# Step one of a two-step graph diffusion: two PSUM copies and the next tile's coarse search levels in another order on ScalarE and GpSimd

## What is computed

```python
def _adj_from_feats(Xa, W1, W2, W3):
    Q = Xa @ W1
    K = Xa @ W3
    logits = Q @ W2 @ K.T / TAU
    idx = jnp.argsort(-logits, axis=1)
    vals = jnp.take_along_axis(logits, idx, axis=1)
    csum = jnp.cumsum(jax.nn.softmax(vals, axis=1), axis=1)
    k_i = jnp.sum(csum < P_NUC, axis=1) + 1          # P_NUC = 0.9
    ...
    masked = jnp.where(keep, logits, -jnp.inf)
    return jax.nn.softmax(masked, axis=1)
...
for s in range(STEPS):                               # STEPS = 2
    A = _adj_from_feats(Xa, W1, W2, W3)
    Xf = Rf @ Xf
    Xb = Rb @ Xb
    Xa = A @ Xa
    Z = Z + (Xf @ U1[s] + Xb @ U2[s] + Xa @ U3[s])
```

## Time and profile before

| what | value |
|---|---|
| median of 3 runs | 2497.32 us (2494.7 to 2497.5) |
| the profiled execution: its own time | 2493.01 us |
| the profiled execution: span | 2491.2 us |
| PE busy | 1956.3 us (79%) |
| DVE busy | 1924.2 us (77%) |
| ACT busy | 1700.4 us (68%) |
| POOL busy | 838.4 us (34%) |
| mean granted TensorE clock | 0.921 of full speed |
| chain that ended last | ACT 21%, issue 13%, POOL 13%, PE 4%, DVE 1% |

### The profile page before, as it was taken

How to read it: one execution, slowest core, us unless ns; L and a number is a source line. 1 busy time by engine, 2 the same in 40 slices (tenths; PEclk the granted TensorE clock), 3 DMA queues, 4 the chain that set the end, 5 groups by cost and what they waited for, 6 DMA issues and landing times.

```text
span 2491.2 us, 33017 instructions
## 1 busy us (share of the span) xinstructions
PE 1956.3 (79%) x10002; PEld 1286.8 (52%) x10002; DVE 1924.2 (77%) x6082; ACT 1700.4 (68%) x1806; POOL 838.4 (34%) x1438
## 2 busy tenths in 40 slices
PE   2999565999999999998548778778778678688693
PEld 1555333666666666666325455445455455455462
DVE  6777658888888888887386887877877878878876
ACT  4434147888888888886367777777777677677640
POOL 2000043444444444444243343333332332333423
PEclk9999887999999999999869989989989989889896
DMA  6777220111111111111510100001001001001013
GB/s 228 286 284 278 103 65 18 49 48 49 49 48 49 48 48 48 48 48 39 180 61 1 39 20 25 34 20 38 20 20 39 20 20 39 20 20 39 19 47 140
DMA packets 65726, 167.62 MB, mean 67 GB/s; under 512 B 7037, under 2 KB 45307, under 8 KB 61947
## 3 DMA queue, kind: packets, MB, share of 16 engines
q1 hardware_dynamic: 65530, 165.43, 19.1%
HBM read 117.95 MB, written 47.45 MB: 66 GB/s over the span
## 4 chain that ended last, share of the span: by engine, by line
ACT 21%; issue 13%; POOL 13%; PE 4%; DVE 1%; POOLq 0%; DMA 0%; ACTq 0%; DVEq 0%; SPq 0%
ACT junk_a L900 10%; ACT junk_a L895 8%; POOL over L808 7%; PE banks L1346 3%; POOL over L816 1%; ACT pt L919 1%; POOL over L811 1%; POOL rough_t L818 1%; POOL points L820 1%; DVE region L1274 1%; POOL minus_t L822 1%; POOL points L814 1%; DVE region L1269 0%; ACT zt L945 0%; PE banks L1338 0%
## 5 line engine op out<-in xcount | busy, mean ns | idle before, releaser
L1346 PE MATMUL banks<-xa,pt 128*128 128x256 f32 x2704 | 683.2, 407 | 232.7 <-ACT pt L919 232.7
L1346 PEld LDWEIGHTS banks<-xa,pt 128*128 128x128 f32 x2704 | 534.0, 204 | 389.1 <-ACT pt L919 245.1
L895 ACT ACTIVATE junk_a<-pb_all,minus_t 128x3327 f16<-128x3327 f32 x151 | 463.9, 3072 | 221.2 <-POOLq L823 220.9
L900 ACT ACTIVATE junk_a<-pb_all,minus_t 128x3327 f16<-128x3327 f32 x151 | 463.0, 3066 | 1.8
L1392 PE MATMUL banks<-region,at 128*128 128x512 f16 x2028 | 448.9, 381 | 0.0
L808 POOL TENSOR_SCALAR over<-over,points 128x1 f32<-128x1 f32 x151 | 104.5, 692 | 881.3 <-ACT junk_a L900 881.2
L1200 DVE TENSOR_SCALAR_CACHE_REDUCE pb_all<-banks 128x1024 f32<-128x1024 f32 x260 | 210.9, 848 | 225.9 <-PE banks L1311 223.7
L1392 PEld LDWEIGHTS banks<-region,at 128*128 128x128 f16 x2028 | 199.1, 98 | 230.1 <-issue 4.1
L1311 PE MATMUL banks<-keys,qs 64*128 64x512 f32 (+1 forms) x832 | 199.9, 577 | 88.4 <-DVE pb_all L1200 49.2
L808 POOL TENSOR_SCALAR over<-over,rough_t 128x1 f32<-128x1 f32 x78 | 185.1, 2373 | 169.2 <-ACT junk_a L900 169.1
L1338 PE MATMUL banks<-ident,pb_all 128*128 128x128 f32 x1352 | 181.6, 281 | 54.5 <-DVE pb_all L1131 34.4
(11 more groups left out here) (222 smaller groups left out, 2859.7 us busy)
## 6 DMA issues: line engine op xcount, KB each, us to landing
at<-adjT_d SPq DMA_DIRECT2D x52, 832.0 KB, 4.8
region<-in_adj_dram SPq DMA_DIRECT2D x25, 1663.5 KB, 8.0
adjT_d<-at SPq DMA_DIRECT2D x26, 832.0 KB, 3.9
fb_d<-fb_sb SPq DMA_DIRECT2D x26, 256.0 KB, 2.0
region<-fb_d SPq DMA_DIRECT2D x2, 3328.0 KB, 19.0
y_d<-y_sb SPq DMA_DIRECT2D x50, 128.0 KB, 1.9
x_d<-pb_all SPq DMA_DIRECT2D x1, 3328.0 KB, 10.4
qs<-q_d SPq DMA_DIRECT2D x104, 32.0 KB, 4.1
```

Of the source, the lines that this page charges most:

```text
L895: nc.scalar.activation(junk_a[:, 0:w], pb[u][:, 0:w], ACT.Relu, scale=sign, bias=t, accum_out=over[u][:, 0:1])\
L900: nc.scalar.activation(junk_a[:, 0:w], pb[u][:, 0:w], ACT.Sign, scale=sign, bias=t, accum_out=over[u][:, 1:2])\
L1346: last = nc.tensor.matmul(bank[4][:, 0:D], pt[sl][:, t * P:(t + 1) * P], xa[:, t0 + t, :], start=(t0 + t == 0), stop=(t0 + t == T - 1))
```

## The change

Two tables and the place of two calls change; all of it is in step one (the entries of step zero stay).

```diff
--- before.py
+++ after.py
@@ -71,7 +71,7 @@
     ROUGH = (0, 3)
     BISECTIONS = (4, 3)
     ACT_BISECTIONS = (3, 3)
-    EARLY_BISECTIONS = (0, 3)
+    EARLY_BISECTIONS = (0, 2)
     AIM = (6.0, 16.0)
     CUT_AIM = (6.0, 24.0)
     VERIFIED = (0, 1)
@@ -853,7 +853,6 @@
                             .then_inc(S2("fb_lo")[k.slot], 1)
                     if not first:
                         level(m, 1)
-                        level(m, 2)
                 step_sweep(pool, body)
                 if not first:
                     pool.wait_ge(sem("scale_in"), 32)
@@ -865,7 +864,7 @@
             def _(act):
                 act.wait_ge(S("search_consts"), 1)
 
-                STEPS = ((), (0,), (1,), (2, 3), (4,), (5,)) if first else ((), (6,), (7,), (8, 9), (10,), (11,))
+                STEPS = ((), (0,), (1,), (2, 3), (4,), (5,)) if first else ((), (4, 5, 6), (7,), (8, 9), (10,), (11,))
                 relus = Chain(act, "step_relu_sum", base=sum(sum(LEVELS[q]) for q in range(s)))
                 signs = {}
 
@@ -967,14 +966,8 @@
                                     .then_inc(S2("sx_lo")[i.slot], 1)
                                 nc.scalar.activation(t256[i.slot][:, n, :], bank[5 + n][:, D:2 * D], ACT.Copy, scale=sc[:, i.t, :])\
                                     .then_inc(S2("sx_lo")[i.slot], 1)
-                                if n == 0 and m.inside(T):
-                                    for q in range(2, 4):
-                                        sums(m, q)
-                    elif not first and m.inside(T):
-                        for q in range(2, 4):
-                            sums(m, q)
                     if not first and m.inside(T):
-                        for n in range(4, 6):
+                        for n in range(2, 4):
                             sums(m, n)
                     if not first and i.static and i.t == T - 1:
                         layernorm_sqrt(act, 2, 0, T - 2)
```

## The result

The changed kernel takes 2532.58 us (median of 4 runs, 2530.62 to 2535.24) against 2497.41 (2494.7 to 2497.89) for the kernel before: 1.0144 times as long, 95% interval 1.0126 to 1.0161, some 35 us more. The direction was forecast; the time lies above the forecast range, which ended at 2529.

The account below looks back on a forecast made before the run. ACT and POOL in turns set the pace. Legs of 27.6 to 28.2 and 18.7 made the period 46.3 to 46.9 against 46.08; over 23 periods 5 to 19, middle 12: 2497.3 + 12 = 2509 us, range 2494 to 2529.

Parts of the forecast that it names:

- the two legs: Period split: first from start of DVE pass L1131 (A) to first fine sum (F), 16.59 us; second F to next A, 28.93.
- F = A + 18.7: First fine sum starts 18.7 us after L1131's start, against 16.59, because POOL's additions and L1064 delay level 2.
- Product 2 starts at F + 4.0: On PE, product 2 starts 4.0 us after the first fine sum's start, following the third `pt` copy at 3.06.
- Products 0 and 1 with their transposes and the first logits ... end near A + 16.7 to A + 18.2: This PE stretch, taken as 10.1 us, ends 16.7 to 18.2 us after L1131's start, before product 2's gap.
- 1.5 or 2.6 us more: Extra time for product 2 on PE if the clock is half after a gap of 5 to 6 us.
- F + 11.9: Third piece of logits reaches DVE 11.9 us after the first fine sum's start, against 15.3; L1131 follows 13.62 later.
- The flag's limit, F + 27.6: DVE's L1155 awaits PE's L1317 behind 52 matmuls, so next L1131 starts at least 27.6 us after the first fine sum.
- "Nothing" for startup and end: Startup and the end of the last tile were forecast to add no time to the total.
- the slower rival: PE's clock also falls ahead of the 52 matmuls L1392: 40 to 65 us more, 2537 to 2562; chance 0.08.
- the faster one: Rival: DVE does not hold POOL's 256-column additions; 30 to 43 us less, about 2460; chance 0.14 together with smaller mistakes.
- Gain and loss: Rival: the two legs' changes cancel within 0.2 us a period, time 2492 to 2502; chance 0.22.
- shorter gaps cost none: Argument against the slower rival: the 8.4 us gap and product 0 account for the period's 6.4 us at half clock.

Follow-up runs that it names:

- e4: Changed kernel with 28 unused matmuls per step-one tile added on PE ahead of the first logits piece, to fill its gap; 2511.8 us.
- e6: e5 with the fourth `pt` copy and the `xo` copy each moved one fine sum earlier; 2427.94 us, 0.974 of the kernel before.
- e7: Changed kernel with POOL's `add_z` and identity addition put behind level 2, the two `spread` additions left ahead of it; 2504.81 us.
- e1: Changed kernel with POOL's order alone put back, level 2 ahead of all four additions; ACT keeps the new order; 2478.99 us.
- e5: Changed kernel with the edits of e1 and e3 together; 2452.43 us, 0.9834 of the kernel before on the same chip.
- e3: Changed kernel with the third `pt` copy moved ahead of the first fine sum (n = 6); 2498.01 us.

## Why the prediction was wrong in size

- **What bounds the kernel, and the two legs:** right. Edits of POOL's order moved the first leg, edits of the copies the second. From tile 3 on the first leg is the same within 0.04 us in every kernel but e4, whose first one is 16.47, and e6, where the meeting behind L1131 is not the same in every tile.
- **"F = A + 18.7":** right. Measured 18.61, in all 23 tiles from 3 to 25 within 0.03. Each part was there: the held short step (0.48), the held pass (0.44), `add_z` held for 3.4 us. e7 and e1 take the leg apart. The one meeting at the last tile was enough to size it.
- **"Product 2 starts at F + 4.0":** this step failed. It started at F + 6.1. I let PE do the first piece of logits in the gap, as in the order of before, where the third copy was long done when PE came to it. That piece writes the PSUM tile from which ACT takes the third copy, so it waits for the copy as well and stands ahead of product 2: 2.1 us with the start of its own. "Products 0 and 1 with their transposes and the first logits ... end near A + 16.7 to A + 18.2" holds the error. I had measured that stretch up to product 2's start (10.1 us) and not looked at what its last piece waits for.
- **"1.5 or 2.6 us more" by the clock:** product 2 itself took 4.80, 1.5 more than 3.29; the piece of logits ahead of it took 0.95 more, which the sum did not have. F + 11.9 + 2.1 + 1.5 is F + 15.5, and 13.6 behind it is F + 29.1; 29.2 was measured. With this term the same sum gives 29.1 + 18.7 = 47.8, the settled period (47.79).
- **The flag's limit, F + 27.6:** right as a limit, but idle in the changed kernel, where PE and DVE came later than it; L1155 waited in tile 2 only, for 1.1 us, and in the last tile, as before. It showed where PE was earlier: in e4 and e5.
- **"Nothing" for startup and end:** off by little. Tile 2's period was 3 us shorter, a gain from the earlier copies (42.7 to 42.8 in e1, e3, e5 and e7 too) that the other tiles lost again. The end is 4.1 us longer: 2.0 by the leg A to F, 0.4 by `xo`, and 1.65 because the last tile's L1385 began at half clock behind an idle stretch of 3.6 us (granted clock 0.50 from 2419.80 to 2421.50; from the `xo` copy to the flag 13.97 us, against 12.32 in the earlier trace rows). There the slower rival, the clock ahead of L1392, did come true.
- **The rivals:** POOL's additions were held, so the faster one fell. Gain and loss did not cancel either: the second leg gained 0.3 us, where 1.3 to 1.9 had been forecast. The slower one decided nothing in the changed kernel's regular part, but it does in seven tiles of e4 and nine of e5. What I held against it, "shorter gaps cost none", was wrong: the clock was at half behind a gap of 2.0 us in the changed kernel (the transposes), and behind 2.6 us in e5 (granted clock 0.50 from 1761.4 to 1764.8).

## What to carry to other kernels

A small engine's operations queue behind each other as well as behind the engine that shuts them out: what stands ahead of the result that others wait for is paid in full, even work of 0.7 us that cost nothing where it stood before. When a copy moves, follow every reader and every writer of its PSUM tile, also those that were never late before; a gap that closes in one place opens ahead of the next one that needs the copy. And try the halves of such a change by themselves: here ScalarE's half alone was a gain of 18 us, and GpSimd's half on top of it a loss of 54.

## What the runs showed of the hardware

POOL and DVE kept out of each other's way operation by operation: a DVE instruction with two SBUF inputs that met a POOL addition of 256 columns took 0.44 to 0.54 us more and went in ahead of POOL's next operation, which then stood until the pass was over (L787 4.10 instead of 0.73). That was the same in tiles 3 to 25 of the changed kernel. The Trainium skill (SBUF — State Buffer, Who interferes with whom) calls the ports that the two engines share an exclusive lock and says: "Issue order, not op shape, decides who blocks." The traces agree; that the turn changes between two operations of a queue is what these rows add.

Not expected was how regular the kinds of period are: 45.71 and 46.45 us in turns before, 47.79 each time in the changed kernel, 45.85, 46.81 and 47.27 in turns in e7, 41.6 and 45.4 mixed in e6. The program gives these tiles the same work and changes only their buffers, in twos and threes, in all of these kernels alike. In the kernel before, product 0 takes 4.80 us in one kind and 5.92 in the other behind the same 8.41 us gap, and these 1.12 us are the difference of the second leg (28.94 against 30.06). Why it takes the one or the other was not tried.
